# One split of an expert weight on VectorE, moved from ahead of phi to between the two statistics instructions of the second layer norm

## The reference, cut to what matters

```python
h = embeddings[x]                                   # 64 x 128 x 256
qkv = layernorm(h) @ W_qkv + b_qkv
pq, pk = phi(q), phi(k)                             # phi(x) = elu(x) + 1
kv = einsum('bshd,bshm->bhmd', pk, v)
z = 1 / (einsum('bshd,bhd->bsh', pq, pk.sum(1)) + 1e-6)
h = h + einsum('bshd,bhmd,bsh->bshm', pq, kv, z)
x2 = layernorm(h)
rw = gating(x2)                                     # 16 experts, two or more kept
q, k, v = (einsum('btc,ech,bte->bth', x2, proj, rw) for proj in (q_proj, k_proj, v_proj))
h = h + einsum('bth,ehc,bte->btc', causal_attention(q, k, v), o_proj, rw)
```

## Time and profile before

| | |
|---|---|
| median of 3 runs | 983.25 us (982.54 to 984.55) |
| profiled execution, its own time | 981.2 us |
| its span | 979.5 us |
| VectorE busy, of the span | 843.0 us (86%) |
| TensorE busy, of the span | 922.2 us (94%) |
| granted TensorE clock, mean | 0.996 |

### The profile page before, as it was taken

The page is one execution under the profiler, slowest core; times in us unless marked ns, Lnnn a source line. Parts: engine busy times, 40 slices in busy tenths (PEclk is TensorE's granted clock), DMA queues, the critical chain, the costliest instruction groups (busy, mean ns, idle before and its releaser), DMA issues.

```text
span 979.5 us, 20631 instructions
## 1 busy us (share of the span) xinstructions
PE 922.2 (94%) x5231; PEld 795.1 (81%) x5231; DVE 843.0 (86%) x2918; ACT 599.7 (61%) x1633; POOL 675.2 (69%) x902
## 2 busy tenths in 40 slices
PE   4999999999989999989899999999999999999998
PEld 3778788887778889889899878888888888888776
DVE  3789999999999987656575579999999999999998
ACT  4566666767666654335444556667666666666664
POOL 5437777777777755199500368888888888888885
PEclk9999999999999999999999999999999999999999
DMA  2114344443334349888988833333333333333331
GB/s 67 50 55 129 119 135 146 148 156 119 123 120 127 101 140 319 284 281 262 293 258 257 254 89 108 100 104 98 105 109 108 104 101 97 105 109 108 94 96 38
DMA packets 106298, 137.54 MB, mean 140 GB/s; under 512 B 13762, under 2 KB 93634, under 8 KB 106180
## 3 DMA queue, kind: packets, MB, share of 16 engines
q1 hardware_dynamic: 88500, 85.03, 27.6%
q0 software_dynamic: 17408, 50.35, 17.4%
q10 hardware_dynamic: 272, 0.79, 0.2%
HBM read 70.06 MB, written 66.06 MB: 139 GB/s over the span
## 4 chain that ended last, share of the span: by engine, by line
PE 38%; DVE 37%; issue 10%; POOL 7%; DMA 4%; ACT 3%; SPq 1%; DVEq 0%; POOLq 0%; ACTq 0%
PE bank L1800 10%; PE bank L1802 10%; PE bank L1801 9%; PE bank L1807 4%; DVE phi L1396 4%; DVE qk_e L1712 3%; DVE x L1712 2%; POOL row_y L924 2%; DVE attn L1339 2%; DVE kvm L1415 2%; DVE w_attn L1737 2%; DVE stats L1352 2%; PE bank L1826 2%; DVE stats L1178 2%; DVE zden L1337 1%
## 5 line engine op out<-in xcount | busy, mean ns | idle before, releaser
L1800 PE MATMUL bank<-wo_hi,split_lo 128*128 128x512 f32 x512 | 214.2, 418 | 5.1 <-issue 4.1
L1802 PE MATMUL bank<-wo_hi,split_hi 128*128 128x512 f32 x512 | 202.9, 396 | 0.0
L1801 PE MATMUL bank<-wo_lo,split_hi 128*128 128x512 f32 x512 | 202.7, 396 | 0.0
L924 POOL DMA_INDIRECT row_y<-sorted_y,pair_now x128 | 128.2, 1002 | 31.8 <-issue 22.0
L1077 ACT ACTIVATE h<-bank,rwo 128x256 f32<-128x256 f32 x256 | 107.0, 471 | 29.6 <-PE bank L1802 20.5
L1800 PEld LDWEIGHTS bank<-wo_hi,split_lo 128*128 128x128 f32 x512 | 97.1, 190 | 24.7 <-issue 4.3
L1802 PEld LDWEIGHTS bank<-wo_hi,split_hi 128*128 128x128 f32 x512 | 96.5, 189 | 23.0
L1801 PEld LDWEIGHTS bank<-wo_lo,split_hi 128*128 128x128 f32 x512 | 97.2, 190 | 17.2
L1712 DVE SCALAR_TENSOR_TENSOR qk_e<-bank,rwo,qk_e 128x256 f32<-128x256 f32 x256 | 110.9, 474 | 0.2 <-PE bank L1802 0.2
L833 POOL TENSOR_TENSOR roots<-roots_in,minus_half 128x3 f32<-128x3 f32 x67 | 59.6, 890 | 73.9 <-DVE roots_in L1361 73.9
L1800 PE MATMUL bank<-wq_hi,split_lo 128*128 x288 | 110.3, 383 | 0.0
(11 more groups left out here) (261 smaller groups left out, 2601.6 us busy)
## 6 DMA issues: line engine op xcount, KB each, us to landing
sorted_y<-w_attn SPq DMA_DIRECT2D x34, 384.0 KB, 3.6
h_rows<-h SPq DMA_DIRECT2D x64, 128.0 KB, 1.7
row_x<-h_rows SPq DMA_DIRECT2D x64, 128.0 KB, 3.6
out_h<-row_x SPq DMA_DIRECT2D x64, 128.0 KB, 2.5
sorted_y<-row_y SPq DMA_DIRECT2D x18, 384.0 KB, 3.1
h<-sorted_x SPq DMA_DIRECT2D x53, 128.0 KB, 2.9
sorted_y<-raw SPq DMA_DIRECT2D x12, 384.0 KB, 3.0
sorted_x<-zeros SPq DMA_DIRECT2D x32, 128.0 KB
```

The costliest lines, as they stand in the source:

```text
L924: pool.indirect_dma_start(out=row_y[:, 2 * tile.p + n, :], out_offset=None, in_=sorted_y[0:LATE_FROM * P, :] if tile.c < KEPT else sorted_ ...
L1800: pe.matmul(ps, left[1][c], right[0][c], start=(c == 0), stop=False)
L1801: pe.matmul(ps, left[0][c], right[1][c], start=False, stop=False)
L1802: last = pe.matmul(ps, left[0][c], right[0][c], start=False, stop=(c == n - 1))
```

## The change

In the first stage, the weight split (L598, 128x256) no longer stands between `centers` and `phi`. `second_stats` is cut in two: `bn_stats` stays there, `bn_aggr` becomes `second_moments`, and the weight split is issued between them. Nothing is added or removed; the one call of `second_stats` in the tail gets its `second_moments` right behind it.

```diff
             def second_stats(tile):
                 after(dve, "h2", tile)
                 dve.bn_stats(stats[:, 2 * tile.p + 1, :], h2[tile.p][:, :]).then_inc(done["ln2_stats"], 1)
+
+            def second_moments(tile):
                 after(dve, "ln2_stats", tile)
                 dve.bn_aggr(moments[:, tile.c + 3, 1, :], stats[:, 2 * tile.p + 1, :]
                             ).then_inc(done["ln2_moments"], 1)
@@
                     gates_formed()
                 if i.c == 0:
                     gate_columns_scaled()
-                for n in weights_at(i.c - 1):
-                    weight_lo(dve, n)
                 if phi_tile.inside(B):
@@
                 if attn_tile.inside(B):
                     second_stats(attn_tile)
+                for n in weights_at(i.c - 1):
+                    weight_lo(dve, n)
+                if attn_tile.inside(B):
+                    second_moments(attn_tile)
                 row = i.c + 5
@@
                     second_stats(Tile(B - 1))
+                    second_moments(Tile(B - 1))
```

## The result

| | before | changed |
|---|---|---|
| median of 4 runs | 983.38 us (982.54 to 984.55) | 993.04 us (991.97 to 993.63) |
| ratio | | 1.011, 95% interval 1.0092 to 1.0128 |
| first to last split of the first stage | 76.3 to 329.4 us | 79.8 to 342.3 us |
| last `x1_lo` of the stage | 354.0 us | 363.7 us |

The change costs 9.7 us by the medians of these runs. The ratio 1.011 would be 10.8 us, and its interval reaches from 9.0 to 12.6 us; both 9.7 and the forecast of 10.2 us (993.4 us) lie in it.

The account below looks back on a forecast made before the run. The prediction took a ring of waits from VectorE to ScalarE and back as the bound: 0 ahead of `phi`, +0.22 us per step behind `bn_stats`, 48 steps less 0.3, taken as 10.2 on 983.25, about 993.4 us; range 988 to 997.

Parts of the forecast that it names:

- The split ahead of phi was free: Between `centers` and `x1_lo`: removing the 0.34 us split gains 0, as VectorE would wait for ScalarE anyway.
- step 56: First-stage step without a split between `centers` and `phi`; `centers` to `x1_lo` is still 1.89 us, as in step 33.
- The new place costs 0.22 us: Between `bn_stats` and `bn_aggr`: the pair grows from 0.45 to 0.67 us, lengthening `x1_lo` to the next `centers`.
- The gap of 0.12 us is real: Between `bn_stats` and its dependent `bn_aggr`: 0.46 us against 0.34 with an independent instruction, so the split can fill 0.12.
- The case by the Trainium skill's rule: Rival at the new place: no gap is filled, the list grows by 0.34 us per step, 999.5 us; chance 0.03.
- The sum of 10.2 us: Over the first stage: 48 x 0.22 = 10.6 us, less 0.3 where the second ring binds, taken as 10.2.
- its own bounds of 0.17 and 0.34: Growth per step at the new place: +0.17 us at the low end, +0.34 if the split fills nothing.
- The delay passes on whole: From first stage to kernel end: the second stage starts from VectorE's results, so all 10.2 us should reach the end.
- the rival that half is given back: End of first stage or second stage: other waits or idle time leave about 5 us, 988.4 us; chance 0.05.
- Nothing on GpSimd: `roots` behind `roots_in`: ends 0.34 us before `centers`, both move together, so no new wait arises.
- What the waits would show: Waits for L1010 of some 0.15 to 0.3 us in each of 48 steps; x1's for `centers` in nearly all.

Follow-up runs that it names:

- experiment 3: The changed kernel with one more copy of the same weight split ahead of `phi`, writing the same values; 991.03 us, ratio 1.0095 to the kernel before.
- experiment 8: The kernel before with one more ScalarE copy of v, read by nobody, ahead of `vx` in the 48 steps; 993.08 us, ratio 1.0132.
- Experiment 1: The kernel before with the weight split moved from ahead of `phi` to right behind `phi`; 992.58 us, ratio 1.011.
- Experiment 2: The kernel before with the weight split moved behind `roots_in`; 996.75 us, ratio 1.0158.
- experiments 5: The kernel before with the first norm's `bn_aggr` moved between the second norm's `bn_stats` and `bn_aggr`, split left ahead of `phi`; 978.42 us, ratio 0.9977.
- experiment 6: The kernel before with the first norm's `bn_aggr` between the second norm's `bn_stats` and `bn_aggr`, and `kvm`'s second instruction between `bn_aggr` and `roots_in`; 976.39 us, ratio 0.9956.
- Experiment 4: The changed kernel with the coming tile's `bn_stats` (L1178) moved, from step 8 on, to right behind `centers` of the next step; 980.65 us, ratio 0.9991.
- experiment 7: The kernel of experiment 6 with ScalarE copying the high part of the turned x1 (L1010) ahead of `vx` (L1002); 996.73 us, ratio 1.0163.

## Why the prediction was right, point by point

- *The split ahead of phi was free.* Right. `centers` to `x1_lo` stayed at 1.88 us without it, experiment 3 put 16 us of work back there at no cost, and experiment 8 lengthened the chain through ScalarE and paid for it one for one. Experiment 1 shows the limit: behind `phi` the same split costs 11.6 us. The control that decided the forecast was step 56.
- *The new place costs 0.22 us.* Nearly right: 0.20 in the step shown (3.63 less 3.43) and by the splits' starts. `bn_stats` to `bn_aggr` was forecast at 0.67 and reads 0.66, in step 33 and on the mean of the 48 steps (before, 0.46 in step 33 and 0.45 on the mean); the split itself runs at a median of 406 ns at its new place and 418 at the old.
- *The gap of 0.12 us is real.* Right. Experiment 2, which doesn't fill it, is 6 us dearer than the change, and experiments 5 and 6 fill it with profit. The case by the Trainium skill's rule in "VectorE: DVE Perf Modes", section "The DRAIN you can't avoid", that a semaphore between chained operations costs nothing extra, would have made the change and experiment 2 equal. The trace does not agree, by 0.12 us. The section also says, without a figure, that an operation which isn't held starts earlier, which the prediction didn't weigh; the 0.33 us from `bn_stats` to the split fits that.
- *The sum of 10.2 us.* It measured 9.7, and was over by the 0.01 to 0.02 us per step above. The times alone can't tell 9.7 from 10.2 (interval 9.0 to 12.6), so that the forecast came within 0.4 us is in part luck. Its range took a growth of 0.20 to 0.26 us per step, narrower than its own bounds of 0.17 and 0.34 and without a reason given; the 0.20 that was measured is at its edge.
- *The delay passes on whole.* Right: 9.7 us at the last `x1_lo` and 9.7 us by the medians. The two profiled executions differ by 12.4 us (981.2 and 993.63); what is beyond 9.7 arises in the later stages and lies within what single runs scatter (977.4 to 983.1 us in 17 runs of the kernel before on one chip). The interval, 9.0 us at least, excludes the rival that half is given back.
- *Nothing on GpSimd.* Right, by experiment 2: the later moments were not what cost. `roots` ends 0.35 us before `centers` on the median, before and after.
- *What the waits would show.* Only half right. I expected the wait for L1010 in each of the 48 steps and that for `centers` in nearly all; the list has them 32 and 14 times. The list reckons idle time from the end of the instruction before, whose record overlaps the next start, so short waits drop out. The distances between starts show them in all 48 steps: `attn` to `x1_lo` is at least 0.50 us, where 0.34 is what it takes without a wait, and x1 starts 0.24 us behind `centers`.
- *Where later expectations failed.* Experiment 4 gained nothing over before, and experiment 7 lost 16 us where I had expected -9. In both, the term left out was TensorE's order: what stands ahead of the turning of x1 in the one, and in the other the product L1908, which came later and for which `kvm` then waited.

## What to carry to other kernels

A filler for a gap behind a dependent pair pays only if it comes from the same bounding stretch; moved in from a place where its engine would have waited, it costs its time less the gap, here 0.34 less 0.13 us in 48 steps. An engine that is busy 94% of a stage can still sit on a ring with others: compare distances from start to start between two fixed points in steps with and without the work in question, since a wait of 0.06 us shows in no list here. And a place inside a stretch that ends in a wait isn't free as such: each ring through it has to be added up by itself.

## What the runs showed of the hardware that had not been expected

Of two instructions of VectorE that don't depend on each other, the second starts about 0.08 us before the first one's recorded end (218.19 + 0.42 to 218.52; mean of the 48 steps 0.08). One that waits for the first starts 0.03 to 0.11 us after that end (`bn_aggr` behind `bn_stats`, `roots_in` behind `bn_aggr`), so a dependent pair leaves room for a small instruction: between `bn_aggr` and `roots_in`, 0.29 us apart with a `bn_aggr` that costs 0.09 elsewhere, a 128x16 instruction of 0.14 us fits without moving either (experiment 6).
